# Expert stage: products kept in PSUM, both inputs in one bank, and a three-pass down low-rank product with its weights side by side

## The reference

```python
scores = softmax(x @ gate_weight.T)
topk_w, topk_idx = jax.lax.top_k(scores, 6)          # of 64
w_dense = zeros((T, 64)).at[rows, topk_idx].add(topk_w)
flat = w_dense[:, inv_mapping]                        # [T, 8 experts, 8]
scalar = flat.sum(-1)
soft = softmax(where(flat == 0, -1e9, flat), axis=-1)

def _fused_linear(x, W, qa, qb, scale, w):
    out = x @ W.T
    a = einsum('th,krh->tkr', x, qa)                  # k = 8, r = 8: 64 low-rank features
    b = einsum('tkr,khr->tkh', a, qb)
    return out + scale[None, :] * einsum('tkh,tk->th', b, w)

def expert(muW, gW, gqa, gqb, gs, uW, uqa, uqb, us, dW, dqa, dqb, ds, w):
    xe = x + w @ muW.T
    gate = silu(_fused_linear(xe, gW, gqa, gqb, gs, w))
    up = _fused_linear(xe, uW, uqa, uqb, us, w)       # 176 wide
    return _fused_linear(gate * up, dW, dqa, dqb, ds, w)
y = einsum('fth,tf->th', outs, scalar) + shared(x)
x = layernorm(x + y)
```

## Time and profile before

| | |
|---|---|
| median of 3 runs | 999.36 us (998.17 to 1001.8) |
| the profiled execution | 1000.12 us |
| its span in the profile | 998.5 us |
| expert stage, from its first input matmul to the end | 582.7 to 998.5 us |
| busy share of the span: PE, PE weight loads, DVE, ACT, POOL | 91%, 79%, 67%, 52%, 38% |

### The profile page before, as it was taken

One profiled execution on the slowest core, in us unless ns is written; L12 is line 12 of the kernel. 1 busy time (PEld: TensorE's weight loads), 2 busy tenths in 40 slices (PEclk: granted clock), 3 DMA queues, 4 the chain that ended last, 5 costly groups with the idle time before them and its releaser, 6 DMA issues. The chain is left out here.

```text
span 998.5 us, 15713 instructions
## 1 busy us (share of the span) xinstructions
PE 906.4 (91%) x5588; PEld 791.6 (79%) x5588; DVE 667.7 (67%) x1315; ACT 518.9 (52%) x1218; POOL 376.8 (38%) x252
## 2 busy tenths in 40 slices
PE   6899999999999997878698978999999999999993
PEld 5799999999999995757577856878787878787882
DVE  4756465565556564657569758777777777778775
ACT  4555574655665553234343436556565556565543
POOL 1721231212221211326215227464656565656420
PEclk9899999999999998889788989999999999999996
DMA  6300000000000001200010112020202020200002
GB/s 222 97 1 22 1 21 11 11 11 11 11 11 11 0 12 49 81 1 1 1 61 8 69 48 74 31 81 24 82 22 83 22 81 21 81 21 22 22 1 85
DMA packets 16428, 37.97 MB, mean 38 GB/s; under 512 B 2048, under 2 KB 6912, under 8 KB 15232
## 3 DMA queue, kind: packets, MB, share of 16 engines
q1 hardware_dynamic: 15744, 35.29, 10.5%
q0 software_dynamic: 640, 2.10, 0.7%
HBM read 34.76 MB, written 2.62 MB: 37 GB/s over the span
## 5 line engine op out<-in xcount | busy, mean ns | idle before, releaser
L234 POOL TENSOR_TENSOR att_probs<-att_probs,att_share 128x512 f32<-128x512 f32 x64 | 66.4, 1039 | 192.1 <-DVE att_share L517 192.1
L1459 POOL TENSOR_TENSOR all_xT_hi<-moe_xe,all_xT_hi 128x1024 fp32r<-128x1024 f32 x31 | 80.7, 2603 | 99.5 <-ACT all_xT_hi L1598 98.6
L421 ACT ACTIVATE att_probs<-att_score,att_bias 128x128 f32<-128x128 f32 x256 | 90.7, 380 | 42.1 <-DVE att_bias L508 41.9
L1467 POOL TENSOR_TENSOR all_xT_lo<-moe_inner,all_xT_lo 128x512 fp32r<-128x512 f32 x64 | 84.3, 1317 | 72.4 <-ACT all_xT_lo L1637 69.0
L1637 ACT ACTIVATE all_xT_lo<-moe_inner 128x512 fp32r<-128x512 f32 x64 | 40.3, 630 | 92.5 <-DVE moe_inner L1707 92.5
L1707 DVE TENSOR_TENSOR moe_inner<-moe_gu,moe_silu 128x512 f32<-128x512 f32 x64 | 43.9, 686 | 62.3 <-ACT moe_silu L1633 58.8
L554 DVE SCALAR_TENSOR_TENSOR att_OT_lo<-att_mix,att_bv,att_OT_hi 128x512 fp32r<-128x512 f32 x64 | 45.9, 750 | 58.8 <-ACT att_OT_hi L459 58.8
L459 ACT ACTIVATE att_OT_hi<-att_mix,att_bv 128x512 fp32r<-128x512 f32 x64 | 43.6, 704 | 66.6 <-PE att_mix L50 66.5
L48 PE MATMUL att_proj<-att_xT_hi,att_Wq_hi 128*128 128x256 f32 x256 | 74.8, 292 | 1.3 <-DVE att_Wq_lo L482 0.5
L48 PE MATMUL att_acc<-att_Wo_hi,att_OT_hi 128*128 128x256 f32 x256 | 73.0, 285 | 1.6 <-DVE att_OT_lo L554 1.6
L295 PEld LDWEIGHTS att_score<-att_KT,att_QT 128*128 128x128 f32 x512 | 63.2, 198 | 12.0 <-issue 9.1
(11 more groups left out here) (298 smaller groups left out, 2923.1 us busy)
## 6 DMA issues: line engine op xcount, KB each, us to landing
all_stage<-in_expert_w SPq DMA_DIRECT2D x8, 1152.0 KB, 5.5
moe_spread<-soft_dram SPq DMA_DIRECT2D x64, 128.0 KB
all_scale<-in_expert_scale SPq DMA_DIRECT2D x8, 320.0 KB, 5.9
att_xT<-in_xT SPq DMA_DIRECT2D x8, 256.0 KB, 3.1
att_stage<-in_Wq SPq DMA_DIRECT2D x4, 512.0 KB, 7.3
att_stage<-in_Wo SPq DMA_DIRECT2D x4, 512.0 KB, 6.2
att_x_tok<-in_x_tok POOLq DMA_DIRECT2D x8, 256.0 KB, 3.1
out<-all_r SPq DMA_DIRECT2D x4, 512.0 KB, 4.4
```

What stands on the lines that cost most here:

```text
L234: pool.tensor_tensor(p3, p3, each, ALU.mult).then_inc(prob_ready, 1)
L421: ins = act.activation(p_[:, c], score[b][:, c], ACT.Exp, bias=bias[b][:, h:h + 1], scale=SCALE, accum_out=m_[:, h:h + 1])
L1459: pool.tensor_tensor(xe[u % 2].lo[:, :], xe32[:, :], xe[u % 2].hi[:, :].bitcast(F32), ALU.subtract).then_inc(xe_lo, 1)
L1467: pool.tensor_tensor(innerT[u % 2].lo[at], inner[at], innerT[u % 2].hi[at].bitcast(F32), ALU.subtract).then_inc(inner_lo, 1)
```

## The change

- `low_product` and `dlow_product` write their result back into `low_bank` and `dlow_bank` instead of SBUF, and every rounding and subtraction that reads them reads the bank.
- ACT writes `low.hi` first and then fills `low_pair` from it; DVE's two half subtractions wait for `low.hi` only.
- A new tile `dq` per weight set holds the 64 + 64 columns of `down_qa`, high and low parts side by side. With these as 128-column weights, `down_low` takes three passes in place of five: high features come out in rows 0 to 63 of the bank, the product with the low weights in rows 64 to 127. Both are multiplied by the spread weights, and `dlow_low` becomes two operations: `dlow_rest` = bank[0:64] - high, then low = bank[64:128] + `dlow_rest`, with a wait between them.
- `dq` costs ACT one copy per weight set ahead of L1620 and POOL one subtraction in `split_low`.
- Both input matmuls write `xe_bank`. PE's order becomes `gate_up`, `down_low`, input 0, `low_rank`, first half of `down`, input 1, second half of `down`. DVE's becomes: `dlow_product`, `xe_sum` 0, `dlow_low`, `low_product`, `xe_sum` 1, `low_low`.

```diff
+def down_qa(w):
+    return w[:, DQ_AT:MU_AT].rearrange("p (k r) -> p k r", k=DK)
+def beside(dq):
+    return dq[:, :].rearrange("p (k h r) -> p k h r", k=DK, h=2)
-def split_low(pool, stage, w, low_done, all_done, count):
+def split_low(pool, stage, w, dq, low_done, all_done, count):
     pool.tensor_tensor(w.lo[:, :], stage[:, :], w.hi[:, :].bitcast(F32), ALU.subtract).then_inc(low_done, 1)
-    pool.wait_ge(low_done, count)
+    pool.wait_ge(low_done, 2 * count - 1)
+    pool.tensor_tensor(beside(dq)[:, :, 1], down_qa(stage), down_qa(w.hi).bitcast(F32), ALU.subtract).then_inc(low_done, 1)
+    pool.wait_ge(low_done, 2 * count)
...
+                    pool.tensor_copy(beside(dq0)[:, :, 0], down_qa(stage))
                     pool.tensor_copy(W0.hi[:, :], stage[:, :]).then_inc(expert_hi, 1)
...
-            def inputs(g, u, slot):
+            def inputs(g, u, k, slot):
                 c = u % CHUNKS
-                for k in range(DK):
-                    pe.matmul(feat[k][:, :], W[slot].hi[0:MR, MU_AT + k * P:MU_AT + (k + 1) * P],
-                              softT[slot][0:MR, c * CT:(c + 1) * CT], start=True, stop=True
-                              ).then_inc(xe_ready, 1)
+                if not (isinstance(g, int) and g == u == k == 0):
+                    pe.wait_ge(xe32_ready, 2 * count(g, u) + k)
+                pe.matmul(xe_bank[:, :], W[slot].hi[0:MR, MU_AT + k * P:MU_AT + (k + 1) * P],
+                          softT[slot][0:MR, c * CT:(c + 1) * CT], start=True, stop=True
+                          ).then_inc(xe_ready, 1)
...
+                        pe.wait_ge(pair_hi, 2 * count(g, u) + n + 1)
                         pe.wait_ge(pair_ready, 2 * count(g, u) + n + 1)
...
-                w, x = W[slot], innerT[u % 2]
-                product(pe, dlow_bank[0:KR, :], w[:, DQ_AT:DQ_AT + KR], x[:, 0:CT], last=False)
-                qa = slice(DQ_AT + KR, DQ_AT + 2 * KR)
-                pe.matmul(dlow_bank[0:KR, :], w.hi[:, qa], x.hi[:, CT:2 * CT], start=False, stop=False)
-                pe.matmul(dlow_bank[0:KR, :], w.lo[:, qa], x.hi[:, CT:2 * CT], start=False, stop=True
+                w, x = dq[slot], innerT[u % 2]
+                both = lambda k: w[:, k * 2 * KR:(k + 1) * 2 * KR]
+                pe.matmul(dlow_bank[:, :], both(0), x.hi[:, 0:CT], start=True, stop=False)
+                pe.matmul(dlow_bank[:, :], both(0), x.lo[:, 0:CT], start=False, stop=False)
+                pe.matmul(dlow_bank[:, :], both(1), x.hi[:, CT:2 * CT], start=False, stop=True
                           ).then_inc(dlow_ready, 1)
...
                     if before:
-
-                        pe.wait_ge(xe32_ready, 2 * count(g, u + (1 if last and u == UNITS - 1 else 2)))
-                        down_low(g, u - 1, (u - 1) // CHUNKS % 2)
+                        down_low(g, u - 1, slot)
+                    if ahead:
+                        if u in (2, CHUNKS + 2):
+                            pe.wait_ge(w_ready, g * 2 + (1 if u == 2 else 2))
+                        inputs(g, u + 2, 0, (u + 2) // CHUNKS % 2)
                     if not (last and u == UNITS - 1):
                         pe.wait_ge(xe_lo, count(g, u + 2))
                         low_rank(g, u + 1, (u + 1) // CHUNKS % 2)
-                    if not (last and u >= UNITS - 2):
...
-                        if before:
-                            pe.wait_ge(dlow32_ready, count(g, u))
-                        inputs(g, u + 2, (u + 2) // CHUNKS % 2)
                     if before:
-                        down(g, u - 1, (u - 1) // CHUNKS % 2, first and u == 1)
+                        down(g, u - 1, 0, slot, first and u == 1)
+                    if ahead:
+                        inputs(g, u + 2, 1, (u + 2) // CHUNKS % 2)
+                    if before:
+                        down(g, u - 1, 1, slot, first and u == 1)
...
-            inputs(0, 0, 0)
-            pe.wait_ge(xe32_ready, 2)
-            inputs(0, 1, 0)
+            for u in range(2):
+                for k in range(DK):
+                    inputs(0, u, k, 0)
...
+                act.activation(low.hi[:, :], low_bank[:, :], ACT.Copy).then_inc(low_hi, 1)
+                act.wait_ge(low_hi, count(g, u + 1))
                 for hi, _, cols in PAIRS:
-                    act.activation(low_pair[hi, cols], low32[hi, :], ACT.Copy).then_inc(pair_hi, 1)
-                act.activation(low.hi[:, :], low32[:, :], ACT.Copy).then_inc(low_hi, 1)
+                    act.activation(low_pair[hi, cols], low.hi[hi, :].bitcast(F32), ACT.Copy).then_inc(pair_hi, 1)
...
+                act.activation(beside(dq[n])[:, :, 0], down_qa(stage), ACT.Copy)
                 act.activation(W[n].hi[:, :], stage[:, :], ACT.Copy).then_inc(w_hi, 1)
...
-                dve.tensor_tensor(low32[:, :], low_bank[:, :], spread[c][:, :], ALU.mult).then_inc(low32_ready, 1)
+                dve.tensor_tensor(low_bank[:, :], low_bank[:, :], spread[c][:, :], ALU.mult).then_inc(low32_ready, 1)
...
-                for n, (hi, lo, cols) in enumerate(PAIRS):
-                    dve.wait_ge(pair_hi, 2 * count(g, u) + n + 1)
-                    dve.tensor_tensor(low_pair[lo, cols], low32[hi, :], low_pair[hi, cols].bitcast(F32), ALU.subtract
+                dve.wait_ge(low_hi, count(g, u + 1))
+                for hi, lo, cols in PAIRS:
+                    dve.tensor_tensor(low_pair[lo, cols], low_bank[hi, :], low.hi[hi, :].bitcast(F32), ALU.subtract
                                       ).then_inc(pair_ready, 1)
...
-                dve.tensor_tensor(dlow32[:, :], dlow_bank[0:KR, :], spread[c][0:KR, :], ALU.mult).then_inc(dlow32_ready, 1)
+                dve.tensor_tensor(dlow_bank[:, :], dlow_bank[:, :], spread[c][:, :], ALU.mult).then_inc(dlow32_ready, 1)
...
-                dve.tensor_tensor(innerT[u % 2].lo[at], dlow32[:, :], innerT[u % 2].hi[at].bitcast(F32), ALU.subtract
-                                  ).then_inc(dlow_lo, 1)
+                dve.tensor_tensor(dlow_rest[:, :], dlow_bank[0:KR, :], innerT[u % 2].hi[at].bitcast(F32), ALU.subtract
+                                  ).then_inc(dlow_rest_ready, 1)
+                dve.wait_ge(dlow_rest_ready, count(g, u + 1))
+                dve.tensor_tensor(innerT[u % 2].lo[at], dlow_bank[KR:P, :], dlow_rest[:, :], ALU.add).then_inc(dlow_lo, 1)
...
+                    ahead = not (last and u >= UNITS - 2)
                     if not (first and u == 0):
                         dlow_product(g, u - 1)
+                    if ahead:
+                        dve.wait_ge(xe_lo, count(g, u + 2))
+                        xe_sum(g, u + 2, 0)
+                    if not (first and u == 0):
                         dlow_low(g, u - 1)
                     if not (last and u == UNITS - 1):
                         low_product(g, u + 1)
-                    if not (last and u >= UNITS - 2):
-                        dve.wait_ge(xe_lo, count(g, u + 2))
-                        xe_sum(g, u + 2)
+                    if ahead:
+                        xe_sum(g, u + 2, 1)
```

78 lines of the change are left out of this document (38 added, 40 removed).

## The result

The changed kernel takes 991.75 us (median of 5, 990.12 to 992.10), the kernel before, run beside it, 998.33 us (median of 5, 997.74 to 1001.8). The ratio is 0.9921 with a 95% interval of 0.9902 to 0.9941. Forecast were 991.5 us, which is a ratio of 0.9921 too. Both kernels once more, in later runs: 992.29 us for the changed one (ratio 0.9932, 0.9912 to 0.9952) and 998.35 us for the one before (0.9997, 0.9982 to 1.0012).

The account below looks back on a forecast made before the run. PE was taken as the bound (busy 351.6 of 366.0 us in the expert stage). Terms +0.3, -13.5, +3.0, +1.5 and +0.8 sum to -7.9 us, from a median of 999.36 to 991.5; range 981 to 998.

Parts of the forecast that it names:

- Step 1: PE's work per turn: down_low goes from 5 passes to 3, so 0.46 us less, from 11.55 to 11.09.
- Steps 2 and 3: Ordinary turns: new PE order and longer chain to dlow_lo; PE stops 0.38 us, period 11.58 against 11.55, nothing gained.
- cover of 0.35 us: Kernel before: L1695 ended at 4.30, down's second half began at 4.65; this cover is less than the two passes removed.
- Step 4: DVE products storing into PSUM banks: taken as 0, bounds from 0.05 us cheaper to 0.10 dearer.
- Step 5: Seven turns after a weight split: PSUM operands keep subtractions at 0.69 us; 81.1 against 94.6, a gain of 13.5 us.
- Rival C: Turns after a split: DVE still stands behind POOL, the 13.5 us gain goes, 1005.0 us; chance 0.06.
- Step 6: Seven rounding turns: 48-row silu 1.09 us late, 12.67 a turn; 88.7 against 85.7, a loss of 3.0 us.
- Step 7: Start and end: one shared input bank loses 1.5 us at the start, three bare dlow_low lose 0.8 at the end.
- A: Every turn: the chain is shorter than PE, turns fall to 11.09, 977.3 us (half of it 984.4); chance 0.14.
- B: DVE chain: PSUM operands are dearer than taken, 0.13 us a turn, 995.3 us; chance 0.16.
- D: Rounding turns: the wait merely moves, input 1 stops PE for xe_sum 0; 991.5 us, chance inside the forecast's 0.58.
- no wait before the input matmuls: Expert turns on PE: a sign that would show the forecast true, the old waits for the dlow product being gone.

Follow-up runs that it names:

- the run with `dlow_lo` first: Reordered variant of the changed kernel (976.69 us), with dlow_lo ahead of the 48-row product in all turns and two banks for the first two chunks' inputs: 985.65 us.

## Why the prediction was right

- *Step 1, two passes less on PE:* the floor is 11.10 (forecast 11.09), shown by the run without the addition. That is 0.49 us a turn less than after.
- *Steps 2 and 3, the chain:* right to 0.02 us in each part; ordinary turns of 11.59 against 11.58. The run with five passes shows that it is the chain, and that nothing is gained in these turns. The cover of 0.35 us that I held against the two passes was read where L1695 was stretched to 1.15; unstretched, in the five-pass run, it is 0.88 (`dlow_lo` done at t = 3.80, asked for at 4.68), which the two passes (0.46) and the second operation (0.73) use up together. In the sum, 15 x 0.02 should be 15 x 0.03 by my own 11.58 and 11.55; measured is +0.5 in place of +0.3.
- *Step 4, DVE storing to a bank, taken as 0:* the median of L1704 is 700 ns where the store to SBUF (L1690) took 683. That is at most 0.017 us for the one store on the chain, well inside the bounds. Not all of it need be the bank: `xe_sum`, whose operands did not change, goes from 670 to 691 in after. The one comparison with DVE's order kept is the low product, which goes from 673 to 682 in the kernel before with that product in its bank, 9 ns.
- *Step 5, the turns after a split:* forecast 81.1, measured 81.2. The size was right, the cause only half told. I gave all of it to the operand in PSUM. The two runs on the low product show that either the bank (with `low.hi` ahead) or the rest of the change gives it all. Rival C, with its 1005, asked for a stretch in spite of the bank; none was seen. In the run with the low product in SBUF the pair was stretched by 1.0 us and the kernel took 992.84, but the third subtraction, the one that C named, started ahead of POOL and kept its 0.69, so what a stretch there would cost in this order is not shown.
- *Step 6, the rounding turns,* is the term that was mis-sized: 88.7 forecast, 90.1 measured, 12.64 to 12.85 each instead of 12.67, and the first 13.41. ACT in the turn of 741.80:

```profile
742.49 0.29 ACT L1635 ACTIVATE all_dq<-all_stage 128x128 fp32r<-128x128 f32 x1
742.68 2.12 ACT L1636 ACTIVATE all_W_hi<-all_stage 128x2304 fp32r<-128x2304 f32 x1
...
747.54 0.59 ACT L1649 ACTIVATE moe_silu<-moe_gu 48x512 f32<-48x512 f32 x1
```

  The silu in the last row above starts 1.23 us late (1.66 us behind gate_up's last matmul at 745.88, where 0.43 is usual), not 1.09. The new ACT copy was taken too dear (0.25; the rounding starts 0.19 after it), the later begin of ACT's queue too small: ACT begins the rounding 0.88 us after the turn's start in after, 0.27 in before. Of the 1.4 us, 0.5 is another slip: I forecast from the one turn of 12.16, while the seven of before have a mean of 12.23 (85.64 in all, not 85.7). The first of them is the longest in both kernels (12.62 and 13.41), since ACT begins the rounding later still (0.86 and 1.60 us after the turn's start).
- *Step 7, start and end:* +1.5 forecast at the start, 11.20 less 9.68 is +1.5 measured, and the variants with two banks there have it back. At the end +0.8 was forecast and +0.9 is measured in the tail, but the second profile of before has a tail of 32.1, so this term is not confirmed.
- *What the sum had not:* the routing stage, costed at nothing, gives 1.3 us. The miss in step 6 (+1.4) and this one (-1.3) cancel. And the forecast starts from a first median of 999.36, while before took 998.33 beside the changed kernel: the change was forecast at 7.9 us and is 6.6 between the medians. The closeness of 991.5 to 991.75 is luck to the extent of these.
- *Rivals:* A did not happen, no overlap shortens the chain. B's extra cost was at most 0.02 us and not 0.13. D is seen just where it was placed, in the seven rounding turns (7 waits, 2.6 us), before a longer wait for `dlow_lo`, and changes nothing; the sign "no wait before the input matmuls" holds outside those turns only.

## What the runs showed of the hardware

Reading from a bank costs DVE nothing over reading from SBUF here. `moe_low_lo` takes 692 ns (median of 32) from the bank and one SBUF operand in after, and 693 from two SBUF operands in the run with the low product in SBUF; the half subtractions take 688 and 686. The Trainium skill, page "VectorE: DVE Perf Modes", section "The TRN2 errata", has two statements on this. The order in its table, a fixed 120 cycles from PSUM against 58 from SBUF, is not borne out here. Its formula for an fp32 tensor_tensor, (N + 151) / 0.96 ns, gives 691 ns for 512 columns and agrees with both.

What does differ is who stands in the way. A DVE operation with two SBUF operands that starts behind a POOL operation lasts until that is done (2.77 us, 5.31 us at most in the routing stage of before, where POOL's subtraction takes 5.15). One with an operand in a bank does not (696 ns at most over 32 for L1686). When DVE is first, POOL waits (2.94 instead of 2.41). The Trainium skill, page "SBUF — State Buffer", section "SBUF: two separate sides", calls the port pair that DVE and POOL share an exclusive lock: the first one in blocks the other for the whole instruction. The rows above agree. What I had not expected is how little decides it: 0.01 us in the one run, one cast of 0.37 us in the other.

The granted clock fell behind PE's long waits at the end of the kernel: to 0.50 behind waits of 2.26 us (before) and 3.08 us (after), each for about 3 us, while it stayed at 1.00 behind the 1.75 us of the five-pass run. So a wait near the end can cost more than its length. What else decides it is open: in the run with `dlow_lo` first it fell behind 1.62 us.

## What to carry to other kernels

When passes are taken from the busiest engine, first work out how late the chain beside it is; here 0.46 us of matmuls were bought with a DVE operation of 0.73 on a chain with 0.88 of cover. That gave nothing in an ordinary turn and cost 12 us in the whole kernel against five passes, until the order was changed. In an engine that works in order, look for the gaps in which it waits for another engine's copy: a step that stands in such a gap is free. Moved out of it, the 48-row product left DVE idle for 0.66 us and made the turn 0.35 us longer. Measure each piece of a combined change by itself: one piece of this one, the low product kept in its bank with `low.hi` ahead, was worth more than the whole.
